# Rows of a two-expert layer grouped by pair of experts, and one copy moved to ScalarE

## The reference, cut to what matters

```python
# stage 1 (state-space layer, chunks of tokens; unchanged by the diff but for one copy)
x = x + layernorm(ssd_layer(layernorm(x)))
# stage 2: 8 experts, each token goes to its two best
xn = layernorm(x)
probs = softmax(xn @ Wg)                       # 8 numbers for a token
top_vals, top_idx = top_k(probs, 2); top_vals /= sum(top_vals)
for e in range(8):                             # tokens that did not choose e count as zero
    h = relu(xn @ W1[e] + b1[e])               # 128 -> 256
    out += score[e] * (h @ W2[e] + b2[e])      # 256 -> 128
x = x + layernorm(out)
```

## Time and profile before

| | us |
|---|---|
| median of 3 runs (lowest, highest) | 952.27 (952.08, 953.75) |
| profiled execution | 948.08 |
| its span in the trace | 946.2 |
| PE busy, share of the span | 779.7, 82% |
| DVE | 751.3, 79% |
| ACT | 684.6, 72% |
| POOL | 581.6, 61% |

### The profile page before, as it was taken

The page is one execution under the profiler, slowest core; times in us unless marked ns, Lnnn a source line. Parts: engine busy times, 40 slices in busy tenths (PEclk is TensorE's granted clock), DMA queues, the critical chain, the costliest instruction groups (busy, mean ns, idle before and its releaser), DMA issues.

```text
span 946.2 us, 24562 instructions
## 1 busy us (share of the span) xinstructions
PE 779.7 (82%) x7544; PEld 647.1 (68%) x7544; DVE 751.3 (79%) x2293; ACT 684.6 (72%) x1596; POOL 581.6 (61%) x832
## 2 busy tenths in 40 slices
PE   3699999999999999999999999986784798848700
PEld 2487877877877777777777777765774687738600
DVE  5677879898998989989899899977854565647876
ACT  4678888887887778877888778752663597739744
POOL 4344434376766757666676666665777777777722
PEclk9999999999999999999999999996797899989955
DMA  7000000000000000000000000062232543364643
GB/s 203 18 2 5 4 3 5 3 18 18 16 18 16 19 16 16 19 18 17 16 20 16 18 17 18 18 170 68 82 90 77 140 110 100 96 207 126 170 134 116
DMA packets 64817, 53.04 MB, mean 56 GB/s; under 512 B 11127, under 2 KB 58515, under 8 KB 64688
## 3 DMA queue, kind: packets, MB, share of 16 engines
q1 hardware_dynamic: 55600, 34.40, 13.5%
q0 software_dynamic: 9088, 17.07, 5.6%
HBM read 26.70 MB, written 25.50 MB: 55 GB/s over the span
## 4 chain that ended last, share of the span: by engine, by line
PE 48%; DVE 16%; issue 10%; ACT 7%; DMA 7%; SPq 5%; POOL 5%; DVEq 1%; POOLq 0%; ACTq 0%
PE bank L859 6%; PE bank L656 5%; PE bank L931 4%; PE bank L658 4%; PE bank L657 4%; POOL expert_results L2025 3%; PE bank L843 3%; PE bank L845 3%; PE bank L914 2%; PE bank L877 2%; PE bank L920 2%; DMA expert_results<-moe_y,moe_dest 2%; SPq L1654 2%; DMA rows<-csplit 2%; PE bank L870 2%
## 5 line engine op out<-in xcount | busy, mean ns | idle before, releaser
L2025 POOL DMA_INDIRECT expert_results<-moe_y,moe_dest x156 | 157.6, 1010 | 49.8 <-issue 42.9
L1305 POOL DMA_INDIRECT expert_rows<-xall,row_index x128 | 138.7, 1084 | 30.9 <-issue 25.3
L1020 POOL TENSOR_TENSOR y<-y,zt 128x256 f32<-128x256 f32 x64 | 46.8, 731 | 140.2 <-issue 88.7
L943 ACT ACTIVATE m<-bank 128x512 f32<-128x512 f32 x128 | 69.2, 592 | 71.6 <-PE bank L845 71.6
L2000 PE MATMUL bank<-moe_w,moe_hid 128*128 x624 | 93.5, 297 | 30.7 <-DVE moe_y L2018 22.3
L656 PE MATMUL bank<-thi,whi 128*128 128x512 f32 x224 | 105.1, 469 | 8.5 <-ACT bt L697 4.4
L2000 PEld LDWEIGHTS bank<-moe_w,moe_hid 128*128 128x128 f32 x624 | 82.3, 205 | 37.5 <-issue 36.2
L1029 DVE TENSOR_TENSOR mg<-bank,m 128x512 f32<-128x512 f32 x128 | 82.4, 685 | 19.8 <-PE bank L859 19.1
L658 PE MATMUL bank<-thi,wlo 128*128 128x512 f32 x224 | 89.7, 401 | 0.0
L657 PE MATMUL bank<-tlo,whi 128*128 128x512 f32 x224 | 89.5, 400 | 0.0
L982 POOL TENSOR_TENSOR ysum<-ysq 128x128 f32<-128x128 f32 x64 | 35.6, 556 | 71.2 <-ACT ysq L966 71.2
(11 more groups left out here) (235 smaller groups left out, 2395.0 us busy)
## 6 DMA issues: line engine op xcount, KB each, us to landing
moe_block_in<-expert_rows SPq DMA_DIRECT2D x78, 132.0 KB, 2.2
rows<-expert_results SPq DMA_DIRECT2D x12, 512.0 KB, 5.1
out_dram<-m SPq DMA_DIRECT2D x16, 256.0 KB, 2.3
expert_results<-moe_y,moe_dest POOLq DMA_INDIRECT x156
expert_rows<-spare_row SPq DMA_DIRECT2D x18, 132.0 KB, 2.8
parts<-csplit SPq DMA_DIRECT2D x128, 4.0 KB
rows<-csplit SPq DMA_DIRECT2D x128, 4.0 KB
expert_rows<-xall,row_index POOLq DMA_INDIRECT x128, 2.5
```

Of the source, the lines that this page charges most:

```text
L943: SE.activation(m[:, hf * HH:(hf + 1) * HH, :], banks[2 + hf][:].rearrange("p (h l) -> p h l", l=P), ACT.Exp).then_inc(m_ready.sem, 1)
L1305: PL.indirect_dma_start(buckets[n], bass.IndirectOffsetOnAxis(row_index[:, k, t:t + 1], 0), xall[:, t, :], None).then_inc(scattered[n], 16)
L2025: PL.indirect_dma_start(back_d, bass.IndirectOffsetOnAxis(dest[:, b % BACK, n:n + 1], 0), yout[:, b % BACK, n, :], None, bounds_check=2 * ...
```

## The change

Rows are grouped by the pair of experts that a token chose (28 pairs), not by expert. Each tile is written once, not twice; the row carries the signed difference of the two best logits (`C_GAP`) instead of a rank. `dve_route_second` makes the pair's number from the two ranks (four more small instructions for a group of 512 tokens), and counts over 28 pairs. POOL makes the gap in four small instructions for a group (`pool_gap`). `SPLIT` is 12.

For every pair, SP writes W1 of both experts and b1 to DRAM once (`sp_pair_weights`, 2064 bytes for a row of 128, in stage 1 behind the row copies of eight groups; b1 is arranged by 15 small instructions of POOL in tile 8). The filling rows now are 29 DMAs of 66 KB to DRAM instead of 2 of 132 KB, between the last row copies and stage 2's loads; the 16 that `sp_append` made during stage 2 are gone.

Stage 2 works in 91 units of 128 rows, 20 of them from the first half. For each unit SP loads rows and 258 KB of pair weights (`sp_load`, `sp_pick`, two values read for a unit); h is made by four fp32 products of 128 columns without a split; ACT clips the even units and DVE the odd ones, each in four instructions; y of both experts is made by four fp32 products and two bf16 products that add b2. DVE mixes the two results and takes the statistics (`dve_mix`), ACT normalises seven units later, POOL adds x and writes the finished 128 rows to the output in one indirect DMA. For every four units there are seven small instructions on POOL, three on ACT and two on DVE. The last pass is gone. PE reads the two experts' numbers for each unit. W1's split in tile 62 is gone; in its place ACT and DVE split b2 in three rounds.

C's second block (c1) is copied by `act_front`, not by `dve_front`.

```diff
-C_TOK, C_RANK, C_BIAS, C_SCALE = D, D + 1, D + 2, D + 3
-BLK = 2 * P
-SPLIT = 11
+C_TOK, C_GAP, C_BIAS, C_SCALE = D, D + 1, D + 2, D + 3
+NPAIR = NE * (NE - 1) // 2
+SPLIT = 12
-BLOCKS = [2 * (b - a) * GT // BLK + NE - 1 for a, b in HALVES]
-NBLK = sum(BLOCKS)
+UNITS = (TOK + NPAIR * (P - 1)) // P
+EARLY = -(-(SPLIT * GT - NPAIR * (P - 1)) // P) // 4 * 4
...
-        if key in ("c0", "c2", "c3"):
+        if key in ("c0", "c1", "c2", "c3"):
...
-        if key == "c1":
-            dve.wait_ge(fr_done.sem, fdone(f, "c1"))
-            if due(f - 2):
-                dve.wait_ge(yy_done.sem, yy_done.of((f - 2) * TG + TG - 1))
-            DVE.tensor_copy(ct[par][:, 1, :], fr.bank("c1")[:]).then_inc(ctd_ready.sem, 1)
...
         for q, n in plan("scatter", g, i):
-            pool_scatter(pl, q, n, 0)
+            if n == 0:
+                pool_gap(pl, q)
+            pool_scatter(pl, q, n)
...
-        for rows_d in buckets:
-            sp.dma_start(rows_d[NE * BUCKET:NE * BUCKET + BLK].rearrange("(n p) c -> p n c", p=P), dummy[:]
-                         ).then_inc(spare_rows, 16)
+        for n in range(NPAIR + 1):
+            sp.dma_start(rows_d[n * BUCKET:n * BUCKET + P], dummy[:]).then_inc(spare_rows, 16)
...
     def act_prepare(act):
         act.wait_ge(loaded, LOADS)
-        SE.activation(w1[:, :, 0, :], w1f[:], ACT.Copy).then_inc(prep_act.sem, 1)
+        SE.activation(b2x[:], b2[:], ACT.Copy).then_inc(b2_act.sem, 1)
+        act.wait_ge(b2_dve.sem, 2)
+        SE.activation(b2x[64:P, :], b2[64:P, :], ACT.Copy).then_inc(b2_act.sem, 1)
+        act.wait_ge(b2_dve.sem, 3)
+        SE.activation(b2p[:].rearrange("p e d -> p (e d)"), b2[:], ACT.Copy).then_inc(b2_act.sem, 1)
...
+    def sp_load(sp, u):
+        n, row = unit_of(u)
+        if u >= IN:
+            sp.wait_ge(added.sem, added.of(u - IN))
+        at, pair = nc.values_load_multi_w_load_instructions(table_i[n][row:row + 1, 0:2], engines=(mybir.EngineType.SP,),
+                                                            min_val=0, max_val=NPAIR * BUCKET)[1]
...
+        sp.dma_start(block_in[:, u % IN, :], rows_d[bass.ds(at, P), :]).then_inc(block_loaded[u % IN], 16)
...
+    def sp_pick(sp, u):
+        if u >= WR:
+            sp.wait_ge(up_done.sem, up_done.of(u - WR))
+            hidden_read(sp, u - WR)
+        p = pair_now.pop(u)
+        sp.dma_start(w1c[:, u % WR, :], pairs_d[bass.ds(p, 1), :, :].rearrange("o p c -> p (o c)")
+                     ).then_inc(picked[u % WR], 16)
...
+        for n in range(2 * FB):
+            mm = PE.matmul(up_at(u)[:, col(n)], w1c[:, u % WR, col(n)], ht[:, (u // 2) % HT, col(u % 2)], start=True,
+                           stop=True, skip_group_check=True)
...
+        for k, e in enumerate(chosen.pop(u)):
+            o = down_at(u)[:, col(k)]
+            PE.matmul(o, thirds[:], b2p[:, bass.ds(e, 1), :].rearrange("p o d -> p (o d)"), start=True, stop=False,
+                      skip_group_check=True)
             for n in range(FB):
...
+        DVE.tensor_scalar(y[:, u % YR, :], o[:, col(0)], w[:, 0, i:i + 1], None, ALU.mult).then_inc(lower_done.sem, 1)
+        dve.wait_ge(lower_done.sem, lower_done.of(u))
+        DVE.scalar_tensor_tensor(out=y[:, u % YR, :], in0=o[:, col(1)], scalar=w[:, 1, i:i + 1], in1=y[:, u % YR, :],
+                                 op0=ALU.mult, op1=ALU.add).then_inc(mixed.sem, 1)
+        dve.wait_ge(mixed.sem, mixed.of(u))
+        DVE.bn_stats(st6[:, u % YR, :], y[:, u % YR, :]).then_inc(stats.sem, 1)
...
+    def pool_out(pl, u):
+        pl.wait_ge(normed.sem, normed.of(u))
+        PL.tensor_tensor(y[:, u % YR, :], y[:, u % YR, :], block_in[:, u % IN, 0:D], ALU.add).then_inc(added.sem, 1)
+        pl.wait_ge(added.sem, added.of(u))
+        pl.wait_ge(token_kept.sem, token_kept.of(u // 4))
+        PL.indirect_dma_start(rows_out, bass.IndirectOffsetOnAxis(token[:, u % IN:u % IN + 1], 0), y[:, u % YR, :], None,
+                              bounds_check=TOK - 1, oob_is_err=False).then_inc(returned[u % YR], 16)
...
     def scalar_program(act):
...
+        for u in range(UNITS + NORM_LAG):
+            if u < UNITS:
+                att.act_tail(act, u)
...
+            if NORM_LAG <= u:
+                act_norm(act, u - NORM_LAG)
```

More of the change, by code:

```diff
@@ L1463, in pool_body @@
             pool_route_norm(pl, q)
-        for q, n in plan("scatter", g, i):
-            pool_scatter(pl, q, n, 1)
+        if isinstance(t, int) and t == 8:
+            pool_pair_b1(pl)
         pool_gate(pl, t, i, g, par, tp)
@@ L1821, in act_prepare, with returns @@
+    root = sig("out_root_steps", 2)
+    coef = sig("out_coefficients")
+    normed = sig("out_normed")
+    added = sig("x_added")
+    returned = [nc.alloc_semaphore(f"moe_rows_returned{n}") for n in range(YR)]
+    def returns(slot, units):
+        return 16 * len(range(slot, units, YR))
     def act_prepare(act):
         act.wait_ge(loaded, LOADS)
-        SE.activation(w1[:, :, 0, :], w1f[:], ACT.Copy).then_inc(prep_act.sem, 1)
-    def dve_prepare(dve):
-        dve.wait_ge(prep_act.sem, 1)
-        DVE.tensor_tensor(w1[:, :, 1, :], w1f[:], w1[:, :, 0, :].bitcast(F32), ALU.subtract).then_inc(prep.sem, 1)
@@ L1848, in after, with unit_of, dve_table @@
+    def unit_of(u):
+        return (0, u) if u < EARLY else (1, u - EARLY)
+    def dve_table(dve, n, half):
+        rows_of = att.rows_of[:, n, :]
+        pair_number, first_row = att.pair_number[:], att.first_row[:]
+        pid, first, wanted, low, high, product, lower, taken1, start, seen = [one[:, k:k + 1] for k in range(10)]
+        at = table_i[n]
         def after(step):
             dve.wait_ge(table.sem, table.of(n, step))
-        if part == 0:
+        if half == 0:
+            dve.wait_ge(att.rows_counted.sem, n + 1)
@@ new lines, in dve_table @@
+            DVE.tensor_tensor(past[:], past[:], unit_rows[:], ALU.mult).then_inc(table.sem, 1)
+            after(9)
+            DVE.tensor_reduce(first, past[:], AX, ALU.add).then_inc(table.sem, 1)
+            DVE.tensor_scalar(mine[:], pair_number, pid, None, ALU.is_equal).then_inc(table.sem, 1)
+            after(11)
+            DVE.tensor_tensor(past[:], mine[:], taken[:], ALU.mult).then_inc(table.sem, 1)
+            after(12)
+            DVE.tensor_reduce(taken1, past[:], AX, ALU.add).then_inc(table.sem, 1)
@@ new lines, in dve_table @@
+            DVE.tensor_tensor(mine[:], mine[:], rows_of, ALU.mult).then_inc(table.sem, 1)
+            return
+        after(14)
+        DVE.tensor_reduce(high, mine[:], AX, ALU.add).then_inc(table.sem, 1)
+        DVE.scalar_tensor_tensor(out=wanted, in0=first_row, scalar=first, in1=taken1, op0=ALU.subtract, op1=ALU.add
+                                 ).then_inc(table.sem, 1)
+        DVE.tensor_scalar(tri_past[:], att.triangle[:], pid, None, ALU.is_le).then_inc(table.sem, 1)
+        after(16)
@@ new lines, in dve_table @@
+        DVE.tensor_scalar(wanted, wanted, float(P), None, ALU.add).then_inc(table.sem, 1)
+        DVE.tensor_scalar(high, high, -float(P), 0.0, ALU.add, ALU.max).then_inc(table.sem, 1)
+        after(19)
+        DVE.tensor_tensor(start, wanted, high, ALU.min).then_inc(table.sem, 1)
+        DVE.tensor_reduce(low, tri_past[:], AX, ALU.add).then_inc(table.sem, 1)
+        after(20)
+        DVE.scalar_tensor_tensor(out=at[:, 0:1], in0=pid, scalar=float(BUCKET), in1=start, op0=ALU.mult, op1=ALU.add
+                                 ).then_inc(table.sem, 1)
@@ new lines, in dve_table @@
+        after(21)
+        DVE.scalar_tensor_tensor(out=product, in0=low, scalar=-1.0, in1=low, op0=ALU.add, op1=ALU.mult
+                                 ).then_inc(table.sem, 1)
+        DVE.tensor_scalar(at[:, 2:3], low, -1.0, float(NE - 1), ALU.mult, ALU.add).then_inc(table.sem, 1)
+        after(23)
+        DVE.scalar_tensor_tensor(out=lower, in0=product, scalar=0.5, in1=pid, op0=ALU.mult, op1=ALU.subtract
+                                 ).then_inc(table.sem, 1)
+        after(25)
+        DVE.tensor_scalar(at[:, 3:4], lower, float(NE - 1), None, ALU.add).then_inc(table.sem, 1)
@@ L1981, in act_hidden @@
[L1981 to L1994 removed]
+        wait_picked(pe, u)
```

1001 lines of the change are left out of this document (495 added, 506 removed).

## The result

The changed kernel takes 996.12 us (median of 4 runs, 992.35 to 999.74) beside 952.17 us for the kernel before (median of 4, 950.82 to 953.75): a ratio of 1.0462, with a 95% interval of 1.0434 to 1.049. It is 4.6% slower. The forecast was 931 us, with a range up to 958. The profiled execution took 992.35 us, its span is 990.4 (before: 948.08 and 946.2).

A forecast was written before the change was run, and what follows sets the result against it. PE paced stage 1, POOL's indirect DMAs stage 2. Step 13 at 721.7 us, 85 units of 2.35 us to 921.5, 3.5 to land: span 925.0, execution 926.9, median 4.2 above: 931 us, range 908 to 958.

The forecast's parts named there:

- POOL waits for none of them: nothing: Stage 1: one scatter less for a tile frees POOL of 1.27 us, but PE waits for none: nothing gained.
- a quarter: Stage 1: of up to 8 us of extra DVE routing work, a quarter reaches PE: +2 us (0 to 8).
- c1's move at nothing: Stage 1: c1's copy going from DVE to ACT lay in a gap, so it was costed at nothing.
- The seam, +7.9: Between the stages: late b2/W2 loads (7.8 us) and b2's split (+1.4) add 9.2 us, less 1.3 before the first product.
- Steps 0 to 12, 48 us: Start of stage 2: 3.7 us a step in a longer chain, 48 us (42 to 55), step 13 at 721.7 us.
- A unit, 2.35 us: Stage 2: POOL's work sums to 2.21 us a unit; taken as 2.35 (2.21 to 2.88), for 85 units 200 us.
- the 2.60 at which the prediction's sum turns: Stage 2: the unit period in us, over the 85 units left, at which the forecast sum turns.
- PE's 1.9 to 2.1: Stage 2: PE's time in us for one unit's 16 fp32-kind instructions, one transposition and two bf16 products.
- The end, 3.5 us: End of the span: time for the last indirect DMA to land, against 4.0 us after POOL's last addition before.
- (a): Stage 2 rival, chance 0.11: POOL's small instructions are dear, 0.65 us each, unit 2.88 us, span 970, median 976.
- (b): Stage 2 rival, chance 0.17: SP or waits between engines pace the unit, 2.6 to 2.7 us, median 952 to 961.
- (c): Rival, chance 0.15: the seam costs little (+2) and nothing slips, units take 2.21 us, span 902, median 908.

The follow-up runs named there:

- the gap's move: Changed kernel with POOL's four small gap instructions moved from the front of a group's first tile to the end of the tile before: 991.49 us (kernel before 952.77).

## Why the forecast was wrong, step by step

- **"POOL waits for none of them: nothing" (stage 1).** This step failed, and with it "a quarter". I asked which engine waits for POOL by name in the list of waits and found PE waiting for rows and for DVE. Behind both stood POOL, which slowed DVE's instructions without any semaphore. And the routing's extra work reached PE almost whole: 0.9 of 1.15 us for a group, 14.9 us at tile 62 alone, where I had 2 and an upper end of 8. I took DVE's share of waits on PE's list for its slack (and read it too high: 11 waits in 64 tiles are one in six, not one in four). DVE's own timeline, without a gap over three tiles, would have told. Of the 1.9 us that a group grew at full clock, the routing alone is worth 0.9, c1's move 0.7 and the gap's place about 0.6. These are 2.2, so they overlap, and no run separates them fully; the last two are how POOL's and DVE's instructions meet. At tile 62 the routing's extra work cost 5.2 of its 14.9 us in the last group's first two tiles, where the changed kernel lost only 1.2; why is open.
- **c1's move at nothing.** Right alone (1.4 us at tile 62, nothing in a group's time), wrong beside the rest of the change (7.6).
- **The seam, +7.9.** Right in the main: +9.8. SP's block of 29 took 14.65 us (13.8 forecast); ACT's first conversion came at 667.70 us, 12.4 after tile 62, where W1's came 4.4 after it in the kernel before: 8.0 later, 7.8 forecast. Taking the block away gave 6.8. This part of the mechanism held.
- **Steps 0 to 12, 48 us.** 51.5, inside the 42 to 55; no run looked into the 3.5 us.
- **A unit, 2.35 us.** 2.67. The mis-sized term is one: 0.26 us before the DMA, read from the earlier trace rows, where the instruction before the DMA was not the one that made its data. It measured 0.79. The addition (0.46), the DMA (1.01) and the 0.03 were right, the small instructions came to 0.39 and not 0.47. The 84 intervals cost 27 us of the 32.9; the rest is that POOL's unit 6 came 7.3 us after step 13, while I had counted six units done by then. The 2.67 us are above the 2.60 at which the prediction's sum turns, so this term alone would have cost the gain.
- **PE's 1.9 to 2.1.** 2.32 once POOL was out of the way; hidden in the changed kernel.
- **The end, 3.5 us.** 9.0 from the last DMA's end. I carried over the end of the kernel before; the drain is 5 us longer here, and the cause is open.
- **Rivals.** (a) was wrong in its cause: small instructions stayed at 0.19 to 0.23 us, where it needed 0.49. (b) named the right period, 2.6 to 2.7, but SP and the waits between engines for it; it was a wait within one engine. (c) did not happen. No rival let stage 1 grow by more than 8 us. The result lies 65 us above the forecast and 38 above the range's upper end of 958; half of the 65 is the unit (32.9), a third stage 1 (21.6). With either one right the result would still have lain outside.

## What to carry to other kernels

Before calling an engine's added work free, look at its own timeline, not at who waits for it: without gaps there, nothing is free, and an engine can be slowed by another with no wait recorded. Price an instruction that reads what its own engine has just written from a row where that is so; put another unit's work in between. And where an engine has a hole later in the same tile, move what nobody needs soon into it: that was worth 1.9% (interval 1.4 to 2.4%) with no change of the work itself. When two executions are compared stage by stage, compare the granted clock first: of the gap's move 1.9 us were left at tile 62, where the groups at full clock gained 0.6 each.

## What the runs showed of the hardware

- POOL's indirect DMA started 0.79 us after POOL's own addition that made its data, and 0.30 us after an earlier instruction when that data was older (0.29 on average with the addition one unit ahead).
- DVE's 128x128 subtraction took 0.29 us alone and 1.35 us when POOL's three two-input instructions stood beside it; four 128x128 scalings took 1.38 and 3.01. The trace lists no wait for it; the instructions only get longer.
- POOL's closing drain ended 3.9 us after the end of a last addition, 3.9 after that of one indirect DMA, 4.5 after that of the last of eight, and 8.8 in the changed kernel. What makes the difference between 4.5 and 8.8 was not found.
- A group of stage 1 took 40.8 to 41.1 us in the changed kernel where the granted clock was 1.00, and 42.0 in the one group where it was 0.96.
